# The last expert's contribution added in two pairs of rows, and the last store in two parts

## The reference

```python
h = gelu(einsum('bsd,edh->besh', x, W1) + b1[None, :, None, :], approximate=False)
out = einsum('besh,ehd->besd', h, W2) + b2[None, :, None, :]
y = einsum('bse,besd->bsd', gates, out)      # 8 experts, hidden 256, top 2 gates per token
x = x + y                                    # the output, (8, 128, 128) fp32, 512 KB
```

## Time and profile before

| what | value |
|---|---|
| time, median of 3 runs | 239.77 us (239.33, 239.77, 240.34) |
| time of the profiled execution | 241.04 us |
| its span, first to last instruction | 239.3 us |
| outside the span | 241.04 - 239.3 = 1.74 us |
| granted TensorE clock over the span | 0.993 of full |
| PE, DVE, ACT, POOL busy | 94%, 69%, 51%, 34% of the span |
| store of one half (256 KB): time of issue, issue to landing | 0.39 us, 2.3 us |

### The profile page before, as it was taken

How to read it: one execution, slowest core, us unless ns; L and a number is a source line. 1 busy time by engine, 2 the same in 40 slices (tenths; PEclk the granted TensorE clock), 3 DMA queues, 4 the chain that set the end, 5 groups by cost and what they waited for, 6 DMA issues and landing times.

```text
span 239.3 us, 6733 instructions
## 1 busy us (share of the span) xinstructions
PE 223.8 (94%) x2534; PEld 171.4 (72%) x2534; DVE 165.1 (69%) x513; ACT 121.8 (51%) x231; POOL 80.3 (34%) x105
## 2 busy tenths in 40 slices
PE   7999999999998999999988689999799999999993
PEld 7447767776755999999876465877567777776773
DVE  1697668757545775559547665988748974799994
ACT  2564366664675556665720367766445266343340
POOL 8493400001061077756341594746600100000000
PEclk9999999999999999999999999999889999999999
DMA  6991351314004012521122110311300000001001
GB/s 197 377 403 40 86 96 49 93 50 141 3 33 133 3 45 57 167 74 40 36 67 66 49 48 2 94 50 51 89 0 4 0 0 0 3 0 47 3 0 44
DMA packets 12451, 16.38 MB, mean 68 GB/s; under 512 B 1428, under 2 KB 9620, under 8 KB 12292
## 3 DMA queue, kind: packets, MB, share of 16 engines
q1 hardware_dynamic: 10068, 12.87, 17.6%
q0 software_dynamic: 1152, 2.24, 3.4%
q10 hardware_dynamic: 1200, 0.85, 1.1%
HBM read 11.31 MB, written 3.95 MB: 64 GB/s over the span
## 4 chain that ended last, share of the span: by engine, by line
PE 73%; DVE 15%; DMA 4%; issue 3%; POOL 2%; ACT 1%; DVEq 0%; ACTq 0%; POOLq 0%
PE ps L1309 12%; PE ps L1297 11%; PE ps L1089 11%; PE ps L1377 7%; PE ps L1387 7%; PE ps L1146 6%; DVE xn L680 5%; PE ps L998 4%; PE ps L1097 3%; DVE mx L698 3%; DVE stats L666 2%; PE ps L1160 2%; DMA xr<-in_x 2%; POOL rstd L372 2%; PE ps L1012 2%
## 5 line engine op out<-in xcount | busy, mean ns | idle before, releaser
L698 DVE TENSOR_REDUCE mx<-ps 128x4 f32<-128x512 f32 x64 | 41.0, 684 | 15.2 <-PE ps L1089 15.1
L523 ACT ACTIVATE PT<-ps 128x512 f32<-128x512 f32 x64 | 35.6, 590 | 24.9 <-PE ps L1097 24.9
L1089 PEld LDWEIGHTS ps<-k,q 32*128 32x128 f32 x512 | 30.6, 186 | 13.6 <-DVE mx L698 10.1
L1089 PE MATMUL ps<-k,q 32*128 32x128 f32 x512 | 36.1, 282 | 4.4 <-DVE mx L698 3.1
L1097 PE MATMUL ps<-q,k 32*128 32x128 f32 x512 | 34.9, 283 | 0.3 <-DVE mx L698 0.3
L1309 PEld LDWEIGHTS ps<-proj,work 128*128 128x128 f32 x256 | 30.7, 192 | 5.7 <-issue 5.7
L644 ACT ACTIVATE work<-ps,fc 128x512 f32<-128x512 f32 x32 | 21.4, 687 | 24.0 <-PE ps L1297 22.5
L1309 PE MATMUL ps<-proj,work 128*128 128x128 f32 x256 | 31.1, 275 | 0.0
L1097 PEld LDWEIGHTS ps<-q,k 32*128 32x128 f32 x512 | 29.2, 186 | 1.8 <-issue 1.6
L408 POOL DMA_INDIRECT moe_y<-ys,tok_i x22 | 22.3, 1014 | 23.5 <-DVE ys L924 11.5
L1297 PE MATMUL ps<-xT,fc 128*128 128x512 f32 x64 | 30.1, 593 | 0.0
(11 more groups left out here) (156 smaller groups left out, 316.2 us busy)
## 6 DMA issues: line engine op xcount, KB each, us to landing
proj<-in_proj SPq DMA_DIRECT2D x1, 2048.0 KB, 12.8
fc<-in_fc SPq DMA_DIRECT2D x8, 256.0 KB, 3.2
slots_x<-xs SPq DMA_DIRECT2D x2, 709.5 KB, 13.0
fc<-in_w SPq DMA_DIRECT2D x8, 129.0 KB, 2.3
proj<-in_w SPq DMA_DIRECT2D x8, 128.0 KB, 2.7
wr<-in_wr SPq DMA_DIRECT2D x1, 913.0 KB, 8.5
xs<-slots_x SPq DMA_DIRECT2D x2, 322.5 KB, 3.9
xs<-slots_x SPq DMA_DIRECT2D x2, 258.0 KB, 2.9
```

Of the source, the lines that this page charges most:

```text
L523: nc.scalar.activation(PT[:, j % PTR, :], ps[:, ST_BANK(layer, j), :], ACT.Exp, scale=SCALE).then_inc(b_done, 1)
L698: nc.vector.tensor_reduce(mx[:, b, 4 * g:4 * g + 4], ps[:, S_BANK(layer, j), :].rearrange("p (k m) -> p k m", m=M), axis=AX, op=ALU.max).t ...
L1089: ins = mm(ps[:, S_BANK(layer, 2 * n + i), P * k:P * k + P], q4[r:r + 32, k, L * b:L * b + L], k4[r:r + 32, k, M * b:M * b + M], start=Tru ...
```

## The change

In step 15 alone (`LAST_IDX`), rows 6 and 7 (`i >= 2`) go into bank 6 instead of bank 2; rows 4 and 5 stay in bank 2. The last product of row 5 adds to a new semaphore, `dn_front`; the last of row 7 adds to `dn_ps` as before. DVE starts rows 4 and 5 on `dn_front`, signals them with the new `x_front`, waits for `dn_ps`, does rows 6 and 7, and signals `x_exp` as before. SP stores rows 4 and 5 on `x_front` and rows 6 and 7 on `x_exp`, 128 KB each, from the same queue. Nothing else is changed: the number of matmuls and of DVE instructions is the same, and there is one DMA more.

```diff
+        dn_front, x_front = sem("dn_front"), sem("x_front")
...
+        LAST_IDX = 2 * E - 1
+        dn_bank = lambda idx, i: LN_BANK[3][1] if idx == LAST_IDX and i >= 2 else DN_BANK[idx % 2]
...
-            for half in range(2):
-                sp.wait_ge(x_exp, E * (half + 1))
-                sp.wait_ge(b2_added, E * (half + 1))
-                sp.dma_start(out.rearrange("(b t) d -> t b d", t=L)[:, 4 * half:4 * half + 4, :],
-                             xr[:, 4 * half:4 * half + 4, :]).then_inc(s_out, 16)
-            sp.wait_ge(s_out, 32)
+            out_rows = out.rearrange("(b t) d -> t b d", t=L)
+            sp.wait_ge(x_exp, E)
+            sp.wait_ge(b2_added, E)
+            sp.dma_start(out_rows[:, 0:4, :], xr[:, 0:4, :]).then_inc(s_out, 16)
+            sp.wait_ge(b2_added, 2 * E)
+            sp.wait_ge(x_front, 1)
+            sp.dma_start(out_rows[:, 4:6, :], xr[:, 4:6, :]).then_inc(s_out, 16)
+            sp.wait_ge(x_exp, 2 * E)
+            sp.dma_start(out_rows[:, 6:8, :], xr[:, 6:8, :]).then_inc(s_out, 16)
+            sp.wait_ge(s_out, 48)
...
-                dve.wait_ge(dn_ps, idx + 1)
+                if idx < LAST_IDX:
+                    dve.wait_ge(dn_ps, idx + 1)
+                else:
+                    dve.wait_ge(dn_front, 1)
...
-                    ins = nc.vector.scalar_tensor_tensor(xr[:, b, :], ps[:, DN_BANK[idx % 2], 128 * i:128 * i + 128],
+                    if idx == LAST_IDX and i == 2:
+                        ins.then_inc(x_front, 1)
+                        dve.wait_ge(dn_ps, idx + 1)
+                    ins = nc.vector.scalar_tensor_tensor(xr[:, b, :], ps[:, dn_bank(idx, i), 128 * i:128 * i + 128],
...
-                        ins = mm(ps[:, DN_BANK[idx % 2], P * i:P * i + P], hT[:, idx % 2, c, P * i:P * i + P], w2[:, e, c, :],
+                        ins = mm(ps[:, dn_bank(idx, i), P * i:P * i + P], hT[:, idx % 2, c, P * i:P * i + P], w2[:, e, c, :],
                                  start=(c == 0), stop=(c == C1 - 1))
+                    if idx == LAST_IDX and i == 1:
+                        ins.then_inc(dn_front, 1)
```

## The result

The changed kernel takes 238.42 us (median of 22 runs), the kernel before 239.32 us (22 runs, new ones among them): 0.90 us less, ratio 0.9962 with a 95% interval of [0.9943, 0.998]. Forecast were 0.91 us less and 238.9 us. The forecast time is 0.4 us above the measured one because its base was: three runs of the kernel before had a median of 239.77 us, 22 have 239.32. The gain is within 0.5% of no change, and the interval keeps it clear of zero.

What follows compares the result with a forecast made beforehand. PE was taken to bound the kernel until its last product, leaving only the tail to gain: 0.48 us (DVE) plus 0.43 (store) makes 0.91, so 239.77 becomes 238.9 us, range 238.1 to 240.1.

Steps and rivals of the forecast that it cites:

- The bound: PE sets the pace until its last product at 235.32 us; everything gainable lies in the tail of about 4 us.
- The front signal is earlier than it can be used: Before rows 4 and 5: signal 0.4 us early, since DVE is still adding step 14; start 0.14 us after that.
- DVE 0.48 us: DVE's last four instructions end at 236.05 instead of 236.53 us, gaining 0.48, bounds 0.26 to 0.53.
- Rival (b): Wait between rows 5 and 6 breaks DVE's row, ending at 236.27; gain 0.69 us, time 239.1, chance 0.08.
- The other bank: Rows 6 and 7 in bank 6: no new PE wait, 32 records keep their 0.112 us; cost nothing, at most 0.05.
- The halved store 0.43 us: Last store of 128 KB lands 1.87 us after issue instead of 2.3; gain 0.43 us, bounds 0.1 to 0.43.
- The sentence that the two stores' data don't meet: In the DMA engines: first store's data end at 236.95 us, the second's start at 237.04.
- Rival (a): Small store lands in nearly a big one's time, so only DVE's part is gained: 0.58 us, time 239.2, chance 0.14.
- The cover over the added issue: SP is free 0.13 us ahead of its second issue, so the added issue hides beside rows 6 and 7.
- The slower rival: Second store queues behind the first, as line 303's loads did, landing after 2.4 to 3.8 us; up to 240.8; chance 0.12.
- The profile's 1.27 us over the median: Profiled execution of the kernel before took 241.04 us, 1.27 above the runs' median; the tail does not explain it.
- The time, 238.9 us: Whole kernel: median of three runs, 239.77 us, less the gain of 0.91; forecast's chance 0.66.

Runs made afterwards that it cites:

- b2_earlier: Changed kernel with one b2 addition moved: one more after step 3, none after step 13; ratio 0.9959 to the kernel before, last product to last landing 2.62 us.
- row_by_row: `b2_earlier` plus step 14 in two pairs of rows from two banks, step 15's rows 6 and 7 signalled singly from own banks; 237.99 us against 239.33 before.
- three_one_sp: Changed kernel with SP storing rows 4 to 6 (192 KB), then row 7 (64 KB); ratio 0.9945 to the kernel before, last product to last landing 2.87 us.
- rows_211: `row_by_row` with three stores from SP: rows 4 and 5, row 6, row 7; last product to last landing 2.46 us, executed once.
- both_late: Changed kernel with both 128 KB stores issued one behind the other when row 7 is done; last product to last landing 3.20 us, executed once.
- three_one_act: `three_one_sp` with the store of rows 4 to 6 issued by ACT; ratio 0.9983 to the kernel before, last product to last landing 3.05 us.
- row_by_row_act: `row_by_row` with rows 4 and 5 stored from ACT's queue; last product to last landing 2.26 us, executed once.

## Why the prediction was right

By its own steps:

- *The bound.* Right. PE sets the time of the last product, everything won is behind it.
- *The front signal is earlier than it can be used.* Right: DVE starts 0.14 us behind the end of step 14's additions. `b2_earlier` and `row_by_row` show the next limit: moving DVE's other work gives 0.05 us, signalling step 14 in pairs and rows 6 and 7 singly gives 0.37 more.
- *DVE 0.48 us.* Right: 1.22 to 0.74. The wait between rows 5 and 6 does not break the row, the four still start 0.26 us apart. Rival (b) is out, for this kernel and where the count is reached in time.
- *The other bank.* Right: 32 records in 3.73 us before and after.
- *The halved store 0.43 us.* Right in kind, 0.42 in size, and the size came out so well partly by luck. A lone store of 128 KB lands after 1.83 us, 0.47 to 0.48 less than one of 256 KB: the prediction took share times length, 0.85 us, for the length of the data, and they last 1.02 us from first piece to last for 256 KB and 0.57 for 128 KB (in exchange the first piece comes after 0.93 us, not 0.96, and the landing 0.36 after the last, not 0.44). The sentence that the two stores' data don't meet was wrong too: they form one block, as the issues stand 0.47 us apart and not 0.52, and one store's data last 0.57 us and not 0.43. Being second cost 0.07 us. Too little for the halving and nothing for the meeting nearly cancel. Rival (a) is out. The Trainium skill's figures (DMA: Bandwidth & Descriptors, "Anatomy of one DMA — SWDGE (gpsimd) path") would have given 0.30 for the halving, an estimate from them, and the measured 0.47 is nearer to the prediction's own row.
- *The cover over the added issue.* Right, but thinner than said: SP was free 0.08 us ahead of its second issue, not 0.13, because row 5's signal releases a wait instruction ahead of the first store and not the store itself, which puts that issue 0.07 us behind row 5 instead of 0.03. In `three_one_sp` and `rows_211`, where SP is still issuing when row 7 is ready, 0.2 us are lost; in the former by the first issue's coming later, in the latter by the last one's.
- *The slower rival.* Out: the second store landed 1.90 us after its issue in the changed kernel and 1.92 in `both_late`, not 2.4 to 3.8. So a close pair on one queue is not enough to make what line 303's loads showed; what made it is not tested.
- *The profile's 1.27 us over the median.* The prediction left them unexplained. The profile of before has a dip of the granted clock, over which it lost 1.5 us against the changed kernel's.
- *The time, 238.9 us.* 0.4 us too high, since its base, the median of three runs, was 0.45 above that of 22. The gain does not depend on it.

## What to carry to other kernels

Behind the last product of a kernel, three things cost time: the instructions between the product and the last store's issue, the bytes of the last store, and the issuing of it. Splitting the end paid here as long as each piece was signalled before its consumer was free, and the pieces were so far apart that the issuing engine was idle when the last one was ready: two stores were better than one, and better than three. Where runs scatter more than the gain, compare the stretch that was changed in the two traces, from an event that the change cannot move, and not the spans; and set the starts of the same instructions against each other to see where the rest arose.

## What the runs showed of the hardware

- A store from SBUF to HBM in pieces of 512 bytes took 2.30 us for 256 KB, 1.83 us for 128 KB and 1.62 us for 64 KB from its issue: the halvings took off 0.47 and 0.21 us, and 1.4 us or so stay. The last of these was the third of three stores on its queue.
- The data of two stores on one queue, issued 0.45 to 0.53 us apart, formed one block, and the last landing was never before the first issue plus 2.30 us, also when the last piece was 64 KB (`three_one_sp`, 2.31). With three stores (`rows_211`) there was a gap ahead of the last.
- Two stores on the queues of two engines, issued 0.20 us apart, had their end reported 0.18 us later than on one queue (`three_one_act`, 3.05 against 2.87); 0.52 us apart they did not (`row_by_row_act`, 2.26 against 2.25).
- A DVE instruction with a wait whose count was reached 0.14 us before started in its usual place, 0.26 us behind its neighbour; one that waited for DVE's own last instruction started 0.10 to 0.14 us after that one's end.
- Consecutive issues on SP were 0.45 us apart at the closest, and where the last signal released a separate wait instruction ahead of the issue, the issue came 0.05 to 0.06 us later.
- A fall of the granted clock to 1.2 GHz for 3.4 us went with 1.5 us more between two profiles; runs whose mean clock was as low as that profile's (0.993), 4 of 22 of the changed kernel, took 1.3 us more than the others.
